# A delta-rule mixer ahead of a mixture of experts: the gate's projection moved behind the heads' outputs, the turned queries between the halves of the inverse's products, and the first expert's waits reordered

## The reference, cut to what matters

```python
q = silu(causal_conv(x @ Wq)); k = silu(causal_conv(x @ Wk)); v = silu(causal_conv(x @ Wv))
gk = -exp(A_log) * softplus(x @ Wgk + dt_bias);  beta = sigmoid(x @ Wb + bb)
q = rope(l2norm(q), 16);  k = rope(l2norm(k), 16)            # 16 heads of 32
def step(S, (q_t, k_t, v_t, g_t, b_t)):                      # one token
    S = S * exp(g_t)
    S = S + k_t outer (b_t * (v_t - k_t @ S))
    return S, q_t @ S
o = scan(step)
g = x @ Wg                                                   # the gate
y = (o * rsqrt(mean(o*o) + eps) * gnorm_w * silu(g)) @ Wo
# experts: top 2 of 8 by x @ gate_w.T; each silu(x @ w1.T) * (x @ w3.T) @ w2.T, weighted and summed
```

## Time and profile before

| | us |
|---|---|
| three timed runs | 1333.56, 1337.51, 1338.15 |
| median | 1337.51 |
| the profiled execution | 1341.97 |
| its span | 1340.1 |
| TensorE busy | 1304.9 (97%), mean granted clock 0.985 |
| VectorE busy | 915.4 (68%) |
| ScalarE busy | 718.3 (54%) |
| GpSimd busy | 24.0 (2%) |

### The profile page before, as it was taken

One profiled execution on the slowest core, in us unless ns is written; L12 is line 12 of the kernel. 1 busy time (PEld: TensorE's weight loads), 2 busy tenths in 40 slices (PEclk: granted clock), 3 DMA queues, 4 the chain that ended last, 5 costly groups with the idle time before them and its releaser, 6 DMA issues.

```text
span 1340.1 us, 23940 instructions
## 1 busy us (share of the span) xinstructions
PE 1304.9 (97%) x9964; PEld 1107.3 (83%) x9964; DVE 915.4 (68%) x1200; ACT 718.3 (54%) x888; POOL 24.0 (2%) x23
## 2 busy tenths in 40 slices
PE   8999999999999999998999999999988999999998
PEld 8899998989999997776677888888865789888887
DVE  4566566776566665675679899899868677555554
ACT  5544444554444443472367777777654455665552
POOL 0000000000000000002000000000011000000000
PEclk9999999999999999898799999999989999999999
DMA  8101010321010011211058999999970145555552
GB/s 297 37 22 46 22 36 21 108 74 37 21 38 28 21 65 64 74 55 65 33 217 324 364 349 346 346 350 345 364 287 16 63 157 189 186 189 189 186 180 89
DMA packets 50367, 197.72 MB, mean 148 GB/s; under 512 B 12128, under 2 KB 20576, under 8 KB 30560
## 3 DMA queue, kind: packets, MB, share of 16 engines
q1 hardware_dynamic: 47936, 187.41, 38.7%
q0 software_dynamic: 2336, 8.91, 1.9%
HBM read 195.78 MB, written 0.52 MB: 146 GB/s over the span
## 4 chain that ended last, share of the span: by engine, by line
PE 89%; DVE 6%; ACT 2%; DMA 2%; issue 2%; SPq 0%; POOL 0%; ACTq 0%; DVEq 0%
PE psum L465 13%; PE psum L435 13%; PE psum L2488 9%; PE psum L1683 8%; PE psum L492 5%; PE psum L2489 4%; PE psum L1706 4%; PE psum L517 4%; PE psum L1686 4%; PE psum L2471 3%; PE psum L1053 2%; PE psum L1709 2%; PE psum L2497 2%; PE psum L2305 2%; PE psum L476 1%
## 5 line engine op out<-in xcount | busy, mean ns | idle before, releaser
L1752 DVE TENSOR_TENSOR arena_r<-ring,arena_r 128x2048 fp32r<-128x2048 f32 x96 | 219.7, 2289 | 29.7 <-ACT arena_r L1746 29.3
L465 PE MATMUL psum<-ring_r,arena_r 128*128 128x256 f32 x1536 | 198.1, 287 | 0.6 <-DVE ring_r L300 0.6
L1746 ACT CAST arena_r<-ring 128x2048 fp32r<-128x2048 f32 x96 | 183.3, 1913 | 14.4 <-PE psum L1686 11.0
L465 PEld LDWEIGHTS psum<-ring_r,arena_r 128*128 128x128 f32 x1536 | 188.6, 191 | 1.2 <-DVE ring_r L300 1.0
L435 PE MATMUL psum<-arena_r 128*128 128x512 f32 x768 | 183.7, 394 | 1.6 <-ACT arena_r L809 1.1
L2488 PE MATMUL psum<-arena_r 128*128 128x512 f32 x512 | 179.3, 396 | 1.1 <-DVE arena_r L2562 1.1
L435 PEld LDWEIGHTS psum<-arena_r 128*128 128x128 f32 x768 | 141.5, 188 | 33.6 <-issue 2.2
L2442 DVE TENSOR_TENSOR arena_r<-ring,arena_r 128x2048 fp32r<-128x2048 f32 x44 | 100.9, 2292 | 62.0 <-ACT arena_r L2437 62.0
L2489 PE MATMUL psum<-arena_r 128*128 128x256 f32 x512 | 142.8, 279 | 0.0
L1683 PE MATMUL psum<-arena_r 128*128 128x512 f32 x512 | 129.5, 395 | 1.3 <-issue 1.3
L2488 PEld LDWEIGHTS psum<-arena_r 128*128 128x128 f32 x512 | 96.1, 188 | 24.4 <-DVE arena_r L2562 1.3
(11 more groups left out here) (344 smaller groups left out, 1898.9 us busy)
## 6 DMA issues: line engine op xcount, KB each, us to landing
ring<-in_stream SPq DMA_DIRECT2D x151, 1024.0 KB, 4.9
arena<-in_ctxT POOLq DMA_DIRECT2D x8, 1024.0 KB, 11.8
arena<-in_ctxT SPq DMA_DIRECT2D x7, 1024.0 KB, 8.7
arena<-in_wk SPq DMA_DIRECT2D x16, 256.0 KB, 3.2
wv_in<-in_wv SPq DMA_DIRECT2D x8, 512.0 KB, 3.5
arena<-in_wq SPq DMA_DIRECT2D x16, 256.0 KB, 2.7
arena<-in_wk SPq DMA_DIRECT2D x16, 128.0 KB, 3.2
arena<-in_wo SPq DMA_DIRECT2D x2, 1024.0 KB, 6.5
```

Of the source, the lines that this page charges most:

```text
L465: last = nc.tensor.matmul(bank[:, q * T:(q + 1) * T], cx[xp][kc // 4][:, c, kc % 4 * P:(kc % 4 + 1) * P], wv_sb[wp][:, c, :], start=c == w ...
L1746: nc.scalar.copy(mwhi[p % MB], ring[k % RING][:, :]).then_inc(moe_hi, 1)
L1752: nc.vector.tensor_tensor(mwlo[p % MB], ring[(BLK_MOE + p) % RING][:, :], mwhi[p % MB].bitcast(fp32), ALU.subtract).then_inc(moe_lo if p < ...
```

## The change

Seven edits in the order of TensorE, ScalarE and VectorE; no instruction is added or removed.

1. `tile_products` is cut in quarters, and projections of the queries' chunks stand between them.
2. `turn_mix(pe, 1, 4)` (queries) goes from before both halves of `cross_inverse` to between them.
3. All four chunks of the gate's projection go from among `cross_inverse` and `head_products` to behind the heads' outputs.
4. The wait for `mix_gs` ahead of the second batch's head products is now one for `dec_exp`.
5. ScalarE's two `gate_act` go behind the squares of the heads' outputs.
6. VectorE does `cross_inverse_dve` before the first `um_dve`.
7. The first `up` waits for four of VectorE's casts (`xg_lo`) instead of eight; `turn_sel` now waits for all eight.

```diff
--- before.py
+++ after.py
@@ -1146,17 +1146,22 @@
             for c in range(C // 2):
                 project_mix(pe, 1, 1, c)
             pe.wait_ge(rope_ready, 1)
-            tile_products(4, range(G // 2))
+            tile_products(4, range(G // 4))
+            project_mix(pe, 1, 1, 2)
+            tile_products(4, range(G // 4, G // 2))
+            project_mix(pe, 1, 1, 3)
             pe.wait_ge(beta_ready, 1)
             place(beta[:, :], 2).then_inc(placed, 1)
-            tile_products(4, range(G // 2, G)).then_inc(kkd_filled, 1)
+            tile_products(4, range(G // 2, 3 * G // 4))
+            for c in range(2):
+                project_mix(pe, 1, 2, c)
+            tile_products(4, range(3 * G // 4, G)).then_inc(kkd_filled, 1)
             pe.wait_ge(nk_ready, 1)
             place(nk[:, :], 3).then_inc(placed, 1)
-            for c in range(C // 2, C):
-                project_mix(pe, 1, 1, c)
-            for cc in range(2, C):
-                for c in range(C):
-                    project_mix(pe, 1, cc, c)
+            for c in range(2, C):
+                project_mix(pe, 1, 2, c)
+            for c in range(C):
+                project_mix(pe, 1, 3, c)
             pe.wait_ge(uc_ready, 1)
             pe.wait_ge(placed_ready, 2)
             for n in range(G):
@@ -1180,21 +1185,17 @@
             cross_rows(ROWS_BANK, halves[1]).then_inc(inv_filled, 1)
             project_whole(2, 2)
             project_whole(2, 3)
-            turn_mix(pe, 1, 4)
             pe.wait_ge(xt_ready, 2)
             pe.wait_ge(dec_exp, 6)
             cross_inverse(INV_BANK, halves[0])
-            project_whole(3, 0)
+            turn_mix(pe, 1, 4)
             cross_inverse(INV_BANK, halves[1]).then_inc(inv_filled, 1)
-            project_whole(3, 1)
-            project_whole(3, 2)
             pe.wait_ge(mix_evac, 3 * C)
             pe.wait_ge(rope_ready, 2)
             head_products(krot, 0).then_inc(kk_filled, 1)
-            project_whole(3, 3)
             pe.wait_ge(um_ready, 1)
             head_products(qrot, 0).then_inc(qk_filled, 1)
-            pe.wait_ge(mix_gs, 2)
+            pe.wait_ge(dec_exp, G)
             pe.wait_ge(xt_ready, 3)
             head_products(krot, 1).then_inc(kk_filled, 1)
             pe.wait_ge(um_ready, 2)
@@ -1242,6 +1243,8 @@
                         last = nc.tensor.matmul(psum[tile_rows(i), BASE[b], cc * P:(cc + 1) * P], xw[:, b, h * DK:(h + 1) * DK],
                                                 pm[:, b * H + h, :], start=True, stop=True)
                 last.then_inc(o_filled, 1)
+            for cc in range(C):
+                project_whole(3, cc)
             for b in range(B):
                 for cc in range(C):
                     nc.tensor.matmul(psum[0:H, BASE[b] + 1, 0:P], C_("sums")[:, (C + cc) * H:(C + cc + 1) * H], sq[:, 1, cc, b, :],
@@ -1324,9 +1327,7 @@
                 nc.scalar.activation(gsT[:, 2 * i:2 * i + 2, :, :], psum[:, MIX_BANK[3] + i, :].rearrange("p (c b t) -> p c b t", c=2, b=B),
                                      ACT.Silu).then_inc(mix_gs, 1)
 
-            gate_act(0)
             silu_mix_act(act, 2)
-            gate_act(1)
             for b in range(B):
                 act.wait_ge(qk_filled, b + 1)
                 heads = qk[:, b * H:(b + 1) * H, :].rearrange("p (c i) t -> p i c t", i=4)
@@ -1335,6 +1336,8 @@
             for b in range(B):
                 act.wait_ge(o_filled, b + 1)
                 nc.scalar.activation(osq[:, b, :, :], bank4(BASE[b]), ACT.Square).then_inc(osq_ready, 1)
+            for i in range(2):
+                gate_act(i)
             for b in range(B):
                 act.wait_ge(ms_filled, b + 1)
                 nc.scalar.activation(oroot[0:H, b * P:(b + 1) * P], psum[0:H, BASE[b] + 1, 0:P], ACT.Sqrt, bias=epst[0:H, 2:3]).then_inc(ms_root, 1)
@@ -1470,8 +1473,8 @@
             conv_mix_dve(dve, 2, 0)
             rope_dve(dve, 1, qrot, 4)
             conv_mix_dve(dve, 2, 1)
+            cross_inverse_dve(dve)
             um_dve(dve, 0)
-            cross_inverse_dve(dve)
             vp_dve(dve)
             um_dve(dve, 1)
             for a in range(NT):
@@ -1651,6 +1654,7 @@
         def gathered_experts_pe(pe):
             def turn_sel(pe):
                 pe.wait_ge(sel_ready, 3)
+                pe.wait_ge(xg_lo, 2 * C)
                 for e in range(E):
                     for b in range(B):
                         o = (e % 2) * T + b * P
@@ -1672,7 +1676,7 @@
             def up(pe, p, t, i, e):
                 pe.wait_ge(moe_hi, p + 1)
                 if t == 0 and i == 0:
-                    pe.wait_ge(xg_lo, 2 * C)
+                    pe.wait_ge(xg_lo, C)
                     pe.wait_ge(xg_ready, 2 * C)
                 if t >= 2:
                     pe.wait_ge(g_hid if i else g_silu, t - 1)
```

## The result

| | before | changed |
|---|---|---|
| median of 11 runs, us | 1338.15 | 1345.42 |
| lowest and highest | 1333.56, 1342.98 | 1340.79, 1350.55 |
| ratio, 95% interval | | 1.0038 (1.0022 to 1.0053) |
| the profiled execution, its span | 1341.97, 1340.1 | 1350.55, 1348.8 |
| mean granted clock | 0.985 | 0.978 |

The account below looks back on a forecast made before the run. The prediction took TensorE's order as the bound (89% of the chain), or other engines where TensorE waits for them. Its terms, 0.3 − 5.2 − 0.3 + 7.7 − 1.1 + 0 = +1.4 us, gave 1338.9 us, range 1333 to 1344.

Parts of the forecast that it names:

- No change beyond 0.5%: Whole kernel: a difference under 0.5% (6.7 us), which a measurement was said not to tell; chance 0.86.
- the standstill among the tile products that is neither filled nor of its old size: Sign in TensorE's tile products that would show the prediction wrong; the old standstill was 2.02 us.
- A: Tile products cut up by query projections: path gets 0 to +1.0 us as the standstill fills or stays; +0.3 taken.
- B: Inverse's products to second `um`, gate out, queries turned between halves: 6.3 or 4.4 us earlier; −5.2 taken.
- C: Solves: untouched, but the 0.61 us standstill ahead of the last one may fall elsewhere; −0.3, bounds −0.6 and 0.
- D: Gate behind the heads' outputs: 7.3 us on the path, 0.8 for half clock, 0.4 saved; +7.7, bounds +6.9 and +8.5.
- E: First expert: `up` waits for four casts instead of eight; −1.1 us, 0 if the jump into the experts' code bounds.
- F: Clock in Wo and behind: half-clock spell may be lost or grow; 0, bounds −1.6 and +1.6 us.
- rival 2: Code loading by the skill's rule: A +1.0, B −4.4, C 0; +1.8 on the sum, 1340.7 us; chance 0.2.
- rival 1: Faster by the clock: head products, gate and Wo shrink if heads' outputs run at full clock; −4.7, 1334.2 us; chance 0.2.
- (3) Gate at half clock: Gate behind the outputs at half clock throughout: 13.7 instead of 8.1 us, +5.6, 1344.5 us; chance 0.08.
- (4) `up` gains nothing: First expert: the jump is the bound, so the earlier `up` saves nothing; +1.1, 1340.0 us; chance 0.12.

Follow-up runs that it names:

- second profile: The changed kernel timed and profiled once more, unedited: 1345.86 us, ratio 1.0030 (1.0010 to 1.0049) against the kernel before; profiled execution 1345.41 us.
- t2_gate: The kernel before with edits 3, 4 and 5 alone, the gate's projection and activation behind the heads' outputs: 1346.41 us, ratio 1.0042 (1.0026 to 1.0058).
- n_before: The kernel before with three quarters of the gate's matmuls left out: 1340.74 us, ratio 1.0008 (0.9994 to 1.0023).
- n_after: The changed kernel with three quarters of the gate's matmuls left out: 1339.37 us, ratio 0.9989 (0.9975 to 1.0004) against the kernel before.
- c_shadow: The kernel before with edits 6, 7, tile products reordered around query projections, gate chunks inside the inverse's second half and the first `um` wait: 1336.96 us, ratio 0.9961.
- u_gate_back: The changed kernel with the gate back where it was (edits 1, 2, 6 and 7 stay): 1339.46 us, ratio 0.9990 (0.9970 to 1.0011) against before.
- s_ahead: The kernel before with four of the queries' projection matmuls moved right ahead of the tile products' standstill: 1340.22 us, ratio 0.9993 (0.9973 to 1.0012).

## Why the prediction was right in kind and short in size

"No change beyond 0.5%" held, by 1.6 us of 6.7; the 1.4 us did not: 5.1 us in the first comparison, 4.0 in the last. One of the prediction's own signs of being wrong came true, the standstill among the tile products that is neither filled nor of its old size (1.20 and 1.07 us for 2.02). And a change of under 0.5% can be told here: the interval of the ratio is 0.3% wide. By steps, measured in the second profile (first in brackets):

| step | forecast | measured |
|---|---|---|
| A, tile products | +0.3 | +0.8 (+1.0) |
| B, to the first solve | −5.2 | −3.9 (−2.5) |
| C, solves | −0.3 | +0.4 (+0.4) |
| D, outputs to Wo | +7.7 | +8.4 (+8.4) |
| E, first expert | −1.1 | −1.7 (−0.5) |
| F, Wo and router | 0 | −0.7 (+1.7) |
| sum | +1.4 | +3.3 (+8.5) |

**B failed by its size, and it is the step that counts.** I took the 7.3 us of the gate for TensorE's work with some cover, and took "the middle, for I see no row that tells the ends apart". There was such a row: the standstill. Chunk 0 lay in its time, and the 1.38 us were what chunk 0 did not fill. That the second half of the inverse's products ends "at 613.7 as now" was one of my two ends, and it is what happens: the standstill's end doesn't move when the gate goes. The table goes from the end of the values' projection to the end of the standstill. Its last two columns have two transfers that fall in this time, a 1 MB block of weights and a 16 KB packet of the instruction queue, in us behind the end of the projection:

| kernel | work of TensorE in between, us | standstill | together | block | packet |
|---|---|---|---|---|---|
| before | 5.6 | 1.38 | 7.01 | 1.3 to 4.9 | 4.6 to 5.5 |
| t2_gate | 3.7 | 3.30 | 6.95 | 1.3 to 4.7 | 4.6 to 5.6 |
| n_before | 4.4 | 2.95 | 7.32 | 1.3 to 5.1 | 5.1 to 6.0 |
| n_after | 3.9 | 3.13 | 7.01 | 1.2 to 4.8 | 4.7 to 5.6 |
| changed, 2nd profile | 3.9 | 3.10 | 6.99 | 1.2 to 4.9 | 4.6 to 5.5 |
| changed, 1st profile | 3.9 | 2.22 | 6.10 | 1.2 to 6.2 | 3.8 to 4.8 |
| c_shadow | 6.1 | 0.93 | 7.04 | 1.3 to 4.8 | 4.7 to 5.6 |

(Before: 613.03 − 606.02 = 7.01, less 1.38. A last packet of the block, 8 KB, comes later in the changed kernel's second profile.) Thirteen of the fourteen profiles lie between 6.8 and 7.3; only the first of the changed kernel is outside. So about 7 us are paid, whether work fills them or not.

The trace tells what the 7 us are made of. The DMA of the kernel before, 606 to 614 us in 40 slices of 0.2 us: one block of weights, and one packet of the instruction queue.

```profile
GB/s 0 0 0 0 0 0 246 82 41 123 287 164 369 492 246 573 492 246 573 410 246 492 123 123 0 0 0 0 0 0 0 0 0 0 0 0 0 0 0 0
q8 instruction: 1, 0.02, 0.7%
```

The end of the values' projection frees a slot of the ring (`blk_used`), and the block for that slot moves from 1.2 or 1.3 us later on. The instruction queue's packet starts at the end of this block's load: within the last 0.4 us of it in twelve of the fourteen profiles, 0.6 us ahead of its end in `u_gate_back`, and 2.4 us ahead of it only in the first profile of the changed kernel, the one with the short 6.10. TensorE goes on 1.3 to 1.5 us after the packet has landed, in all fourteen. The standstills of the tile products and of the solves and outputs end in the same way, 1.2 to 1.6 us behind the landing of a packet. There, with no block of weights in the way, the packet starts 0.6 to 1.7 us after TensorE has passed the record 127 places ahead of the standstill; here it starts 2.1 to 4.1 us after it. So TensorE stood here for code, and the code's packet went behind a load of weights. An estimate from these numbers: with the packet 1.05 us behind that record (604.14 in the changed kernel's second profile), on its way for 0.95 us and TensorE going on 1.45 us later, it would go on at 607.6, and it stood from 607.4; nearly all of the 3.10 us is then the block's load. No run holds that load back, so this part is read from the traces and not tested.

What the gate gave back here is what lay behind the 7 us: chunks 1 and 2, 5.3 us at a mean clock of 0.68, 3.7 us at full. The rest of B's shortfall is the clock. The head products ran at full before. In the five profiles with all or three quarters of the gate gone from there (both of the changed kernel, `t2_gate`, `n_before`, `n_after`) most of them run at half: the 64 records that took 2.07 us before take 3.5 to 3.8 (clock of the second window 0.94 before, 0.50 and 0.55 in the changed kernel). The two `um` come behind 2.09 and 3.80 us of products instead of 1.70 and 3.40 in my lower end. The 1.70 was misread: in that row the granted clock is 1.00 up to 627.35 and 0.50 only behind it, and 32 head products all at half take 2.09. The second stage gets 1.4 us longer although a chunk of the gate has left it. That chunk, too, had been free: it stood in TensorE's wait for `um`, 1.88 us of which are now open.

**A** took the upper of its two bounds. The pieces did not fill the standstill: 1.20 us of it stayed, at the same place in the count of TensorE's records. Before: 128 + 32 (the placement) + 56 = 216 records from the first tile product; changed: 64 + 2 + 64 + 2 + 32 + 52 = 216; `c_shadow`: 128 + 32 + 32 + 8 + 16 = 216. The second standstill, counted from the end of the values' projection: 4 + 128 + 8 + 59 = 199 before, 200 in the changed kernel and in `t2_gate`, 199 in `n_before` and `c_shadow`. From the first standstill to the second it is 635 or 636 records in each of them, five times 127, and neighbouring standstills in the solves and outputs are 127 or 128 records apart.

This is what rival 2 said: code loading by count. The rule of the Trainium skill, Advanced Engine Details and Errata, section ISA Cache (16 KB lines of 256 instructions), agrees with it: the place is fixed in instructions, whatever their work. The trace agrees with the size of a line, since 127 or 128 records, each with its weight load, are 254 to 256 instructions. The page gives no price for it; the 7 us are from the profiles here.

**D** was cheaper in the gate and dearer beside it. 32 records took 7.5 us, not 8.1: only their start is at half clock. But the outputs ahead of it took 4.8 us (643.88 − 639.10) instead of 3.4: a standstill of 0.61 us now parts two of their records from the other 62. Under **C** I had foreseen that the 0.61 us ahead of the last solve may fall elsewhere, and counted a gain. It does fall elsewhere: the 32 records of the gate (not 64, as the prediction has it) no longer lie ahead, so the place that was behind the 34th of the last solve's 64 records is now behind the second record of the outputs. The 0.75 us are 127 records ahead of it. The table's load was covered as forecast:

```profile
652.08 1.28 ACT L1343 ACT_TABLE_LOAD   x1
653.38 0.36 ACT L1343 ACTIVATE arena<-psum,epst 16x128 f32<-16x128 f32 x1
```

The first root follows its load at once, as in the earlier trace rows, and both lie before the end of the second sums at 655.04. From sums to Wo it takes 6.2 us instead of 6.6.

**E** was right, with a gain somewhat larger than forecast; **F** is chance here: half clock spells in Wo and the router that one profile has and another doesn't.

The stated range was narrower than its own terms. From the sum of 1338.9, the low ends with rival 1 give 1332.3 and the high ends of all six terms 1344.2; with the 2 us of scatter that the prediction names it would have been 1330 to 1346.

**The rivals.** (1) Faster by the clock: fell, the outputs still run at half. (2) Code loading, +3.2 us, had A +1.0, B −4.4 and C 0 against +0.8, −3.9 and +0.4: nearer than my forecast in each of its three terms, and given half its chance. (3) Gate at half clock: fell, 7.5 us instead of 13.7. (4) `up` gains nothing: fell, by 1.5 to 1.7 us in the profiles of seven kernels (0.5 in the changed kernel's first).

**What stays open.** The free 5.6 us of `n_before` have at least three causes, the standstill that opens (1.6 us), the two further ones in the solves (1.1 us) and the clock that falls; no run here separates them. No run holds the block of weights back behind the code's packet, which by the estimate above would be worth up to 3 us in the changed kernel. Why the first profile of the changed kernel has half clock spells that the second lacks isn't known. And `c_shadow` holds four edits at once, which no run takes apart. In its profile the first stage is 4.1 us shorter than before, the second 0.4 longer and the experts 1.6 shorter; the filled first place brought nothing in `s_ahead`, and part of the 4.1 us is a clock that `s_ahead` has as well.

## What to carry to other kernels

Before a piece of work is moved off a busy engine's path, ask what it costs where it stands: leave it out there, and see whether the time falls. Here the gate's matmuls stood in a standstill and in a wait for VectorE, were free in sum, and cost their full length where TensorE had neither. A gap without a releaser that lies at the same count of instructions in two versions is worth a look at the instruction queue in the DMA view: if a packet lands shortly ahead of its end, the engine waits for code. Put work ahead of such a gap and none behind it that could have gone there, and look what else the DMA queues carry when the packet is due.

## What the runs showed of the hardware that was not expected

- TensorE stood still after 216 and after 199 to 200 records, 635 or 636 apart, and the second time it went on about 7.0 us after the preceding projection, with 3.7 to 6.1 us of work in between. `s_ahead`, with 2 us of wide matmuls ahead of the first place, has no standstill there.
- Each of these standstills, and those in the solves and outputs, ends 1.2 to 1.6 us behind the landing of one 16 KB packet of the instruction queue, in all fourteen profiles. The packet that is due while a 1 MB block of weights moves starts at that block's end in twelve of them (before: block to 610.9, packet from 610.6 to 611.6, TensorE on at 613.03).
- Taking 5.6 us of matmuls out of an engine that is 97% busy gave 1.0008 (0.9994 to 1.0023). Without them the standstill grew and the granted clock was lower in the second stage (0.66 for 0.94); in `c_shadow` it is 1.00 through both stages, and in `s_ahead`, with the gate at its old place, too.
